# A six-layer attention and feed-forward stack: rotation tables by halves on GpSimd, and the second gate product, a table load, a pair and a block of matmuls moved in their engines' orders

## The reference

```python
def attn_layer(x, Wqkv, qs, ksc, Wo):
    q, k, v = jnp.split(x @ Wqkv, 3, -1)        # 16 heads of 64, inner width 1024
    q = l2norm(sh(q)) * qs
    k = l2norm(sh(k)) * ksc
    q = q * cos * scale + rotate_half(q) * sin * scale
    k = k * cos * inv + rotate_half(k) * sin * inv
    out = local_attention(q, k, sh(v))          # windows of 32, each sees itself and the one before
    return out @ Wo
def ffn_layer(x, g, bln, W1, b1, W2, b2):       # inner width 341
    xn = (x - mu) / jnp.sqrt(var + 1e-05) * g + bln
    a, gate = jnp.split(xn @ W1 + b1, 2, -1)
    return a * jax.nn.gelu(gate, approximate=False) @ W2 + b2
for i in range(6):
    x = attn_layer(shift_tokens(x), ...) + x
    x = ffn_layer(shift_tokens(x), ...) + x
```

## Time and profile before

| what | us |
|---|---|
| median of 3 runs | 1973.81 (1972.79 to 1976.53) |
| the profiled execution's own time | 1982.47 |
| its span in the trace | 1980.7 |
| TensorE busy in the span | 1643.8 |
| VectorE busy | 1277.5 |
| ScalarE busy | 923.0 |
| GpSimd busy | 750.6 |

### The profile page before, as it was taken

How to read it: one execution, slowest core, us unless ns; L and a number is a source line. 1 busy time by engine, 2 the same in 40 slices (tenths; PEclk the granted TensorE clock), 3 DMA queues, 4 the chain that set the end, 5 groups by cost and what they waited for, 6 DMA issues and landing times.

```text
span 1980.7 us, 42335 instructions
## 1 busy us (share of the span) xinstructions
PE 1643.8 (83%) x17341; PEld 1101.0 (56%) x17341; DVE 1277.5 (64%) x2385; ACT 923.0 (47%) x1681; POOL 750.6 (38%) x1058
## 2 busy tenths in 40 slices
PE   3005576998778899899998999899987999999999
PEld 1002354675545556656655656656654677667576
DVE  6847674213857787878877878788863666666311
ACT  1034132332334556556655656556553666666232
POOL 0000030100256666656765756656740333334000
PEclk6556797899879999999999999999998999999999
DMA  3000002010043433423423433342321000000111
GB/s 106 20 4 0 3 1 61 22 33 14 1 129 95 132 82 91 128 73 100 134 77 88 126 97 98 97 105 84 89 54 43 1 1 2 1 1 1 33 33 32
DMA packets 73806, 113.38 MB, mean 57 GB/s; under 512 B 16086, under 2 KB 36156, under 8 KB 73582
## 3 DMA queue, kind: packets, MB, share of 16 engines
q1 hardware_dynamic: 72798, 110.43, 20.1%
q10 hardware_dynamic: 816, 0.24, 0.1%
HBM read 83.98 MB, written 27.50 MB: 56 GB/s over the span
## 4 chain that ended last, share of the span: by engine, by line
PE 60%; DVE 27%; ACT 6%; issue 5%; DMA 1%; DVEq 1%; POOL 0%; ACTq 0%; POOLq 0%; SPq 0%
PE PS L1387 8%; PE PS L1115 6%; PE PS L1106 6%; PE PS L1576 4%; PE PS L2066 4%; PE PS L2020 3%; PE PS L2045 3%; PE PS L1624 3%; PE PS L1490 3%; DVE st_t L1430 2%; DVE st_ss L1435 2%; DVE st_r L1422 2%; PE PS L1516 2%; DVE al_hist L459 1%; PE PS L1600 1%
## 5 line engine op out<-in xcount | busy, mean ns | idle before, releaser
L1463 POOL TENSOR_TENSOR st_r<-st_r,st_t 128x512 f32<-128x512 f32 x192 | 243.6, 1274 | 261.2 <-DVE st_t L1430 261.2
L1387 PE MATMUL PS<-st_wqkv,st_xs 128*128 128x512 f32 x576 | 304.1, 612 | 16.3 <-DVE st_xs L1637 9.3
L2151 POOL TENSOR_SCALAR la_p<-la_p,la_rden 128x589 f32<-128x589 f32 x64 | 112.8, 1763 | 246.0 <-DVE la_rden L2170 246.0
L1478 POOL TENSOR_TENSOR st_r<-st_r,st_gy 128x512 f32<-128x512 f32 x192 | 196.6, 1056 | 3.8
L1422 DVE TENSOR_TENSOR st_r<-PS,st_rot 128x512 f32<-128x512 f32 x192 | 129.9, 677 | 90.3 <-ACT st_sqh L1406 89.9
L2164 DVE TENSOR_REDUCE la_nmx<-PS 128x1 f32<-128x589 f32 x128 | 92.7, 766 | 91.8 <-PE PS L2028 91.8
L2126 ACT ACTIVATE la_p<-PS,la_nmx 128x589 f32<-128x589 f32 x128 | 95.1, 748 | 106.5 <-DVE la_nmx L2164 106.5
L1174 ACT ACTIVATE m_h<-PS 128x512 f32<-128x512 f32 x128 | 76.4, 598 | 142.3 <-PE PS L1106 142.3
L1406 ACT ACTIVATE st_sqh<-PS 128x512 f32<-128x512 f32 x192 | 114.3, 595 | 58.9 <-PE PS L1387 58.9
L1199 DVE SCALAR_TENSOR_TENSOR m_y<-PS,m_g,m_y 128x128 f32<-128x128 f32 x112 | 31.5, 344 | 161.0 <-PE PS L1115 161.0
L1430 DVE TENSOR_TENSOR st_t<-PS,st_rot 128x512 f32<-128x512 f32 x192 | 130.6, 680 | 0.0
(11 more groups left out here) (312 smaller groups left out, 3491.0 us busy)
## 6 DMA issues: line engine op xcount, KB each, us to landing
st_v_out<-st_v SPq DMA_DIRECT2D x48, 512.0 KB, 2.6
st_vv<-st_v_out SPq DMA_DIRECT2D x96, 256.0 KB, 3.8
st_vv<-st_v_out SPq DMA_DIRECT2D x96, 192.0 KB, 4.7
st_wqkv<-in_st_wqkv SPq DMA_DIRECT2D x18, 512.0 KB, 5.8
m_w<-in_m_w SPq DMA_DIRECT2D x32, 256.0 KB, 3.1
st_vv<-st_v_out SPq DMA_DIRECT2D x72, 64.0 KB, 1.9
st_wo<-in_st_wo SPq DMA_DIRECT2D x6, 512.0 KB
st_w<-in_st_w SPq DMA_DIRECT2D x6, 341.0 KB
```

Of the source, the lines that this page charges most:

```text
L1387: pe.matmul(PS[:, 2 + m % 2, :], self.xs[:, b, P * t:P * t + P], self.wqkv[:, l % 2, k, 512 * half:512 * half + 512], start=True, stop=Tru ...
L1463: pool.tensor_tensor(r, r, self.t2[:, c % 2, :], ALU.add).then_inc(self.added, 1)
L1478: pool.tensor_tensor(r, r, y[:, 8 * c:8 * c + 8].unsqueeze(2).broadcast_to([P, 8, D2]), ALU.mult)\
L2151: pool.tensor_scalar(self.p[:, v % 2, 0, :], self.p[:, v % 2, 0, :], self.rden[:, v % 4, 0:1], None, ALU.mult).then_inc(self.scaled0, 1)
```

## The change

1. The rotation tables are made on GpSimd (`pool_tables`), one half of two operations at a time: for the first layer ahead of its loop, for later layers the q half between the second and the third addition of the last tile of the layer before, the k half behind that tile's four scalings. VectorE waits for each half ahead of product c = 0 and c = 2 (`rot_ready` now counts halves).
2. The pair (L1440, L1442) leaves `dve_proj` and becomes `dve_guess`, placed behind `dve_down` and ahead of `dve_max`. Only in rounds with T % 4 = 2 does something stand between its old place and its new one.
3. TensorE: the mix stands ahead of block 1 of `pe_up` instead of behind it.
4. ScalarE: the load of the Exp table stands behind the copies of groups 2 and 3 of `act_turn_r` instead of ahead of them.
5. VectorE in rounds with T % 4 = 1: gate product 0 ahead of the sum instead of behind it, gate product 1 behind the division instead of ahead of it.

```diff
                     if t == 3:
-                        sp.wait_ge(self.rot_ready, l + 1)
+                        sp.wait_ge(self.rot_ready, 2 * l + 2)
                         self.load_qks(sp, l + 1)
...
-            if c == 0 and T % (B * self.TILES) == 0:
-                self.dve_tables(dve, l)
+            if c % 2 == 0 and T % (B * self.TILES) == 0:
+                dve.wait_ge(self.rot_ready, 2 * l + 1 + k)
...
-            if c == 3:
-                ss, y = self.ss[:, t % 2, :], self.gy[:, t % 2, :]
...
+        def dve_guess(self, dve, T):
+            t = T % self.TILES
+            ss, y = self.ss[:, t % 2, :], self.gy[:, t % 2, :]
+            dve.wait_ge(self.ss_done, 5 * T + 4)
+            dve.tensor_scalar(ss, ss, 1e-24, -0.5, ALU.max, ALU.mult).then_inc(self.ss_done, 1)
+            dve.wait_ge(self.ss_done, 5 * T + 5)
+            dve.tensor_scalar(y.bitcast(I32), ss.bitcast(I32), -0.5, GUESS, ALU.mult, ALU.add)\
+               .then_inc(self.guess, 1)
+
+        def pool_tables(self, pool, l, k):
+            pool.wait_ge(self.qks_in, l * 16 + 16)
+            for j in range(2):
+                ins = pool.tensor_tensor(self.rot[:, k, j, :, :], self.base[:, k, j, :, :],
+                                         self.qks[:, k, j, :].unsqueeze(1).broadcast_to([P, 4, D2]), ALU.mult)
             ins.then_inc(self.rot_ready, 1)
-            dve.wait_ge(self.rot_ready, l + 1)
...
                 pool.tensor_tensor(r, r, self.t2[:, c % 2, :], ALU.add).then_inc(self.added, 1)
+                if c == 1 and following:
+                    self.pool_tables(pool, following, 0)
...
+            if following:
+                self.pool_tables(pool, following, 1)
...
                     self.pe_turn_r(pe, T + 1, 0)
+                if here:
+                    self.pe_mix(pe, T)
                 if end_of is not None:
                     self.pe_up(pe, end_of, 1)
-                if here:
-                    self.pe_mix(pe, T)
...
-                if norm_of is not None or end_of is not None:
-                    self.act_table(act, ACT.Exp)
                 if turn:
                     self.act_turn_r(act, T + 1, 2)
                     self.act_turn_r(act, T + 1, 3)
+                if norm_of is not None or end_of is not None:
+                    self.act_table(act, ACT.Exp)
...
+                if turn:
+                    self.dve_guess(dve, T + 1)
                 if here:
                     self.dve_max(dve, T)
...
+                if end_of is not None:
+                    self.dve_gate(dve, end_of, 0)
                 if here:
                     self.dve_sum(dve, T)
-                if end_of is not None:
-                    self.dve_gate(dve, end_of, 0)
                 if lead:
                     self.dve_proj(dve, T + 2, 1)
+                if here:
+                    self.dve_out(dve, T)
                 if end_of is not None:
                     self.dve_gate(dve, end_of, 1)
-                if here:
-                    self.dve_out(dve, T)
```

More of the change, by code:

```diff
@@ L1436, in dve_proj @@
                .then_inc(self.ss_done, 1)
-            if c == 3:
-                ss, y = self.ss[:, t % 2, :], self.gy[:, t % 2, :]
-                dve.wait_ge(self.ss_done, 5 * T + 4)
-                dve.tensor_scalar(ss, ss, 1e-24, -0.5, ALU.max, ALU.mult).then_inc(self.ss_done, 1)
-                dve.wait_ge(self.ss_done, 5 * T + 5)
-                dve.tensor_scalar(y.bitcast(I32), ss.bitcast(I32), -0.5, GUESS, ALU.mult, ALU.add)\
-                   .then_inc(self.guess, 1)
-        def dve_tables(self, dve, l):
-            dve.wait_ge(self.qks_in, l * 16 + 16)
-            if l > 0:
-                dve.wait_ge(self.qk_used, 32 * l)
-            for k in range(2):
-                for j in range(2):
-                    ins = dve.tensor_tensor(self.rot[:, k, j, :, :], self.base[:, k, j, :, :],
-                                            self.qks[:, k, j, :].unsqueeze(1).broadcast_to([P, 4, D2]), ALU.mult)
+        def dve_guess(self, dve, T):
[11 more added lines that the diff above has]
+                                         self.qks[:, k, j, :].unsqueeze(1).broadcast_to([P, 4, D2]), ALU.mult)
             ins.then_inc(self.rot_ready, 1)
-            dve.wait_ge(self.rot_ready, l + 1)
         def pool_proj(self, pool, T):
             t = T % self.TILES
+            l, last = divmod(T + 1, B * self.TILES)
+            following = l if last == 0 and l < DEPTH else None
             for c in range(4):
@@ L1888, in pool @@
                 pool.wait_ge(self.set_up, k + 1)
+            pool.wait_ge(self.c_in, 48)
+            for k in range(2):
+                self.pool_tables(pool, 0, k)
             for T in range(self.N):
```

## The result

| | before | changed |
|---|---|---|
| median of 13 runs each, measured together | 1978.79 us (1972.79 to 1988.90) | 1966.18 us (1954.01 to 1977.98) |
| ratio | | 0.9932, interval 0.9907 to 0.9957 |
| the profiled execution's own time | 1982.47 | 1977.98 |
| its span | 1980.7 | 1976.2 |

The change makes the kernel 0.7% faster, about 13 us. The forecast was 22.3 us, 1.1%, and the median lies 3 us above the range. The direction was right, the size almost twice too large. Of the 14.7 us between 1966.18 and the forecast of 1951.5, 9.7 are gain that did not come. The other 5.0 are the base: the forecast was taken off 1973.81, the median of 3 runs, and that of 13 is 1978.79. The profiled execution of the changed kernel is its slowest run and gains 4.5 us only, so what follows reads rounds, not the span.

The account below looks back on a forecast made before the run. In rounds 20 to 22 the bound was taken to be a loop through ScalarE and VectorE, not TensorE. Moves 12.8 plus tables 9.5 gave 22.3 us off 1973.81: 1951.5 us, range 1946 to 1963.

Parts of the forecast that it names:

- Round 20, the table load: Rounds with T % 4 = 0: TensorE gets 1.0 us back, the tile's last square and VectorE's loop come 0.43 us late.
- Round 21: Gate products reordered: block 2 waits only for gate product 1, gain there 1.1 to 1.2 us, shifted copy 1.2 early.
- rival E: Round 21: second gate product too late, paid in each of 11 rounds, time about 1979; chance 0.07 with all slower cases.
- Rival B: The loop through ScalarE and VectorE gives gain back: moves worth 2 to 8 us, time 1956 to 1964; chance 0.20.
- The tables: Table rounds behind the first layer: GpSimd hides the table operations, 5 x 1.91 = 9.5 us saved, 0.73 us per operation.
- the moves: Reordering in the stack's rounds: 10 triples at 1.2 us plus about 0.8 for the last, 12.8 us saved.
- Rival C: GpSimd becomes the bound in table rounds, price at most 7.5 us, time 1959; chance 0.05.
- The sum against the time: Whole kernel: 12.8 + 9.5 = 22.3 us taken off the present time, giving 1951.5 us.
- The base: The time before the change from which the 22.3 us were subtracted: 1973.81 us.
- rival D: The table part alone pays and the moves are neutral: time 1964 to 1968; chance 0.04.
- Rival F: No change: unexplained TensorE stops within a block, 3.13 us in round 23, seven more would cost the gain; chance 0.04.

Follow-up runs that it names:

- e2: The kernel before with only the rotation tables moved to GpSimd by halves: 1976.42 us, ratio 0.9951 to the kernel before.
- e1: The changed kernel with the rotation tables back on VectorE, all else kept: 1983.25 us against 1984.64 before, ratio 1.0001.
- e7: The changed kernel with the Exp table load put back ahead of the copies of groups 2 and 3: 1959.11 us in one execution.
- e10: The changed kernel with the Exp table load back ahead of the copies, run for the time: 1953.87 us, ratio 0.9846 to before.

## Why the prediction was wrong

**Round 20, the table load: right.** Product c = 0 of round 21 starts 5.60 us into the round before and after, and round 20 grew by 0.39, forecast 0.43. The scores start 1.13 us earlier in the round (13.14 against 14.27), forecast 1.0. That the 1.0 us is given to TensorE, which is not the bound in this place, and the 0.43 taken from the loop that is, stands in the prediction; that the part as a whole loses was not drawn from it. It loses 0.4 in round 20 and 0.7 in round 21 and gives back 0.1 in round 18: 1.0 us per triple that the change could have had besides.

**Round 21: right to a tenth.** The timeline of VectorE and TensorE in the changed kernel, the successor of the earlier trace rows:

```profile
993.97 0.69 DVE L1422 TENSOR_TENSOR st_r<-PS,st_rot 128x512 f32<-128x512 f32 x1 [2.93 <-ACT st_sqh L1406]
...
995.77 0.74 DVE L1721 SCALAR_TENSOR_TENSOR st_hid<-PS,st_sv,st_gel 128x512 f32<-128x512 f32 x1
...
997.85 0.63 DVE L1422 TENSOR_TENSOR st_r<-PS,st_rot 128x512 f32<-128x512 f32 x1
...
999.58 1.21 DVE L1591 TENSOR_TENSOR st_on<-PS,st_rden 128x1024 f32<-128x1024 f32 x1
1000.71 0.74 DVE L1721 SCALAR_TENSOR_TENSOR st_hid<-PS,st_sv,st_gel 128x512 f32<-128x512 f32 x1
...
1001.50 1.09 PE L1704 MATMUL PS<-st_xfn,st_w 128*85 128x512 f32 x2 [0.63 <-DVE st_hid L1721]
...
1008.84 0.74 DVE L1734 SCALAR_TENSOR_TENSOR x<-PS,st_sv,x 128x512 f32<-128x512 f32 x1
...
1010.51 0.18 DVE L1443 TENSOR_SCALAR st_ss<-st_ss 128x32 f32<-128x32 f32 x1
```

From product c = 0 to gate product 0 1.80 us (forecast 1.80), to the division 5.61 (5.59), to block 2 7.53 (7.5), and TensorE waits 0.63 us for gate product 1 (0.6). Block 2 is thus 1.15 us earlier than before, once the 0.4 of round 20 is taken off. Rival B, the loop giving part of it back, and rival E, the second gate product too late, did not occur. The pair, 0.89 us ahead of `dve_down` before, takes 0.3 behind the copy. Three rounds gained 1.37 us, forecast 1.2: 13.7 for the ten, not 12.0.

**The tables: right.** The timeline of GpSimd in round 22 and the source line of the tables in the changed kernel:

```profile
1018.87 1.42 POOL L1452 TENSOR_TENSOR st_rot<-st_base,st_qks 128x256 f32<-128x256 f32 x2
```

```profile
L1452 POOL TENSOR_TENSOR st_rot<-st_base,st_qks x24: 716/728/902, 570.3 to 1322.4; 128x256 f32<-128x256 f32 x24
```

0.73 us was the value read off the line between 32 and 512 columns. Round 22's kind is as long as round 18's (16.31 and 16.26) and 2.16 us shorter than before. 0.31 of that is the gain that round 18 has too, so the tables brought 1.85 per layer, forecast 1.91: 9.3 us in the sum for 9.5, and the moves 14.8 for 12.8. Rival C, GpSimd as the bound, did not occur. The rule of the Trainium skill that the prediction cites (GPSIMD Engine Reference, Performance versus the Vector engine), about twice as long for two inputs on GpSimd, is near what the trace shows, 0.73 us against 0.41 to 0.46 on VectorE, and costs nothing where GpSimd's time isn't on the path.

**The sum against the time: this step failed.** "Sum. 12.8 + 9.5 = 22.3 us" was taken off the time whole, as if what lies beside the rounds were the same before and after. Undisturbed it is 24.1; the excess grew by 12.1 in the profiles, and the timed gain is 13. The growth of the excess is the term that the prediction put at nothing.

**The base: this step failed too.** 1973.81 was the median of 3 runs of a kernel whose single executions lie between 1972.79 and 1988.90; the 13 have 1978.79, 5.0 us more. The upper end of the range stood for a gain of 10.8 us, and the 12.6 of the medians is more than that. From the better base the same range would have held the time, but by luck: a gain of 24.1 and a loss of 12.1 that was not foreseen. Luck of the same kind is that the time lies where rival D had it, 1964 to 1968 with the moves neutral. The times alone even look like D (e2 9.7 us faster, e1 not at all), but e1's undisturbed rounds are 7.9 us shorter.

**The rival that came nearest.** Rival F named the pauses and their size ("Seven more such stops than before would cost the whole gain (22.3 / 3.13), four the gain of the moves"). Its sentence "Nothing ties them to the order of the work" is what the runs refute. They are tied to it by the count of instructions ahead of them, by how fast the order lets TensorE issue, and, as far as the DMA shares tell, by which transfers it puts beside the end of a count. The new pause at matmul 2734, 3.70 us of the 9.9 by which the pauses grew, stands at a place and a pace that the kernel before has too (4.53 us for the 256 instructions there, 4.56 here). What differs is the DMA share in the 3 us behind the end of the count before, 0.24 there and 0.44 here. 0.04 was far too little for a case of which half came true, and as a term with an uncertainty of its own, some 10 us to either side, it would have carried the range past 1966. Shown is that the pauses end with the arrival of instructions, where they lie, and that a hidden padding without other effect on a round moves the time by up to 16 us. Not settled is whether the data transfers are the cause, since no run moved them alone; why matmul 1983 has a pause of 1.33 us before and 3.00 now at DMA shares of 0.88 and 0.92; and how much of the growth belongs to the shorter rounds.

## What to carry to other kernels

Before a sum of saved tenths is taken off the time, look how far the present time is from the sum of its undisturbed rounds, and what fills the difference: here 33 us of pauses and their half clock, more than the change was worth. Take the base from as many runs as the result will have: 3 runs were 5 us off here. Where an engine stops inside a block of equal instructions for "issue", count its instructions in 256s, and look at the DMA share just ahead; a few small hidden instructions at the front show in one run whether the place matters, and a before and an after are only comparable over several such shifts, each timed in several runs. And an operation moved behind another to serve the engine that is busiest is paid for by the chain that waits for it: ask of each moved part alone which of the two ends the round.

## What the runs showed of the hardware

- TensorE stood for up to 4.6 us at 193 or 194 of a count of 256 of its own stream, and went on 1.2 to 1.6 us after the end of a packet of 16,384 bytes of the instruction queue. Stretches at half clock often follow (20.5 us of rounds 0 to 45 in the kernel before, 30.7 in the changed one, 10.2 in the changed one padded by 64).
- Where 256 instructions were issued in 2.5 to 4.0 us, 70 of 75 ends of a count had a pause when the DMA engines were over 70% busy, and none of 34 when they were under 30% busy.
- Single executions of this one-core kernel lie up to 12 us from their median, while undisturbed rounds repeat to 0.1 us. e7 and e10 are the same kernel, 8.9 us apart: 2.7 us of that lie in rounds 0 to 45, with pauses of 31.1 and 31.7 us, and 4.6 us behind them, with 27.3 and 37.5 us at half clock. Over the 18 profiles the part behind round 45 takes 511.4 to 520.5 us, about 0.4 us more for each us that it spends at half clock.
- Four two-input operations of VectorE took 3.17 us where two of them lay beside GpSimd's scalings and 4.61 where all four did, against 0.41 each at their shortest.
